# Attention's reciprocal as a logarithm and an exponential, and one vector-matrix product moved from TensorE to VectorE

## The reference

```python
q = xt @ Wq.T                                   # keys and values are q too
scores = scale * einsum('bhqd,bhkd->bhqk', qh, qh)
logits = (scores * cmask + (1.0 - cmask) * NEG) * rmask
attn = softmax(logits, axis=-1)
ctx = einsum('bhqk,bhkd->bhqd', attn, qh)
x = x + transpose(ctx @ Wo.T)
```

## Time and profile before

| | |
|---|---|
| median of 3 runs | 1603.24 us (1598.74 to 1605.35) |
| span of the profiled execution | 1599.3 us (its only time; the runs' median lies 3.9 us above) |
| TensorE, GpSimd, VectorE, ScalarE busy | 95%, 84%, 75%, 55% |
| mean granted TensorE clock | 0.981 |

### The profile page before, as it was taken

The page is one execution under the profiler, slowest core; times in us unless marked ns, Lnnn a source line. Parts: engine busy times, 40 slices in busy tenths (PEclk is TensorE's granted clock), DMA queues, the critical chain, the costliest instruction groups (busy, mean ns, idle before and its releaser), DMA issues. The chain is left out here.

```text
span 1599.3 us, 32587 instructions
## 1 busy us (share of the span) xinstructions
PE 1513.2 (95%) x10636; PEld 1185.6 (74%) x10636; DVE 1198.6 (75%) x2676; ACT 877.7 (55%) x2189; POOL 1336.3 (84%) x1078
## 2 busy tenths in 40 slices
PE   5789999999999999999999999999999999999985
PEld 4568777777777777777777777777777777777753
DVE  4487787878778787877878787787878778787753
ACT  4345556565655656565565656556565655656441
POOL 3377989898898989889898988989898898988875
PEclk9779999999999999999999999999999999999998
DMA  4423444544444454444445444444554444454411
GB/s 137 104 65 96 108 120 109 130 123 111 118 113 117 112 130 123 110 118 115 116 113 130 123 110 119 114 117 111 130 123 111 119 113 117 111 130 96 111 53 55
DMA packets 93809, 179.07 MB, mean 112 GB/s; under 512 B 24704, under 2 KB 24832, under 8 KB 93632
## 3 DMA queue, kind: packets, MB, share of 16 engines
q1 hardware_dynamic: 64448, 109.71, 29.2%
q0 software_dynamic: 29184, 67.17, 14.9%
HBM read 36.77 MB, written 33.55 MB: 44 GB/s over the span
## 5 line engine op out<-in xcount | busy, mean ns | idle before, releaser
L835 ACT ACTIVATE small_Pt<-scores,small_kbias 108x270 f32<-108x270 f32 x1280 | 550.9, 483 | 343.7 <-PE scores L1245 334.8
L985 DVE TENSOR_REDUCE small_mxp<-max_scores 108x1 f32<-108x270 f32 x1280 | 546.7, 435 | 250.7 <-PE max_scores L1226 228.9
L646 POOL TENSOR_TENSOR small_Pacc<-small_Pacc,small_Pt 108x540 f32<-108x540 f32 x384 | 520.8, 1356 | 122.3 <-ACT small_Pt L835 116.6
L1226 PE MATMUL max_scores<-small_ops 128*108 128x270 f32 x1280 | 420.1, 336 | 22.2 <-DVE small_mxp L985 21.6
L1257 PE MATMUL ctx_psum<-small_Pt,small_V 108*64 108x270 f32 x2560 | 317.5, 395 | 0.0
L1017 DVE RECIPROCAL small_rsum<-small_rsum 128x67 f32<-128x67 f32 (+1 forms) x512 | 240.8, 532 | 66.3 <-ACT small_rsum L771 66.3
L1242 PE MATMUL scores<-small_ops 128*108 128x270 f32 x1280 | 281.1, 294 | 8.7 <-ACT small_Pt L835 7.0
L1226 PEld LDWEIGHTS max_scores<-small_ops 128*108 128x108 f32 x1280 | 221.3, 175 | 89.9 <-issue 38.4
L1257 PEld LDWEIGHTS ctx_psum<-small_Pt,small_V 108*64 108x64 f32 x2560 | 187.4, 139 | 109.0 <-issue 4.6
L1245 PE MATMUL scores<-small_ops 128*108 128x270 f32 x1280 | 265.4, 289 | 0.0
L1242 PEld LDWEIGHTS scores<-small_ops 128*108 128x108 f32 x1280 | 193.5, 174 | 38.4 <-ACT small_Pt L835 20.1
(11 more groups left out here) (129 smaller groups left out, 2273.2 us busy)
## 6 DMA issues: line engine op xcount, KB each, us to landing
small_ops<-small_H SPq DMA_DIRECT2D x512, 135.0 KB, 2.5
small_ops<-small_L SPq DMA_DIRECT2D x256, 135.0 KB, 2.5
small_ops<-small_mrow SPq DMA_DIRECT2D x128, 2.1 KB
small_xg<-x_rows,small_idx POOLq DMA_INDIRECT x80, 3.9
small_xtail<-x_rows,small_idx POOLq DMA_INDIRECT x80, 5.0
out_rows<-small_xtail,small_idx POOLq DMA_INDIRECT x80, 3.7
out_rows<-small_xg,small_idx POOLq DMA_INDIRECT x80, 4.1
wqT_sb<-wqT SPq DMA_DIRECT2D x1, 1024.0 KB, 5.4
```

The lines of the kernel that those rows point to most:

```text
L646: nc.gpsimd.tensor_tensor(acc, other, t["Pt"][:R, p0], ALU.add).then_inc(pacc_step, 1)
L835: nc.scalar.activation(t["Pt"][:R, (NT * s + k) % f.NP, half, :], ST[(2 * (NT * h + k) + half) % 3][:R, 0:H], ACT.Exp, bias=t["kbias"][:R, ...
L985: nc.vector.tensor_reduce(t["mxp"][:R, h % 2, m // 2, m % 2:m % 2 + 1], MX[m % 2][:R, 0:H], AX.X, ALU.max).then_inc(mx_red, 1)
L1226: nc.tensor.matmul(MX[m % 2][:R, 0:H], ops[:, OPA, tile_cols(m // 2)], ops[:, OPB, half_cols(m % 2)], start=True, stop=True).then_inc(mx_r ...
```

## The change

Two things are changed in the `small` and `middle` forms.

The reciprocal 1/(s + tiny) becomes exp(-ln(s + tiny)) on ScalarE, two instructions, followed by a Newton step on VectorE: the product of the estimate with the sums, written back to the bank, then (product - 2) times the estimate. The sign that this leaves is taken out by the scale, whose two halves become scalar_tensor_tensor with -1. The misc bank of the sums is released by VectorE's second instruction instead of ScalarE's copy. One activation table set that holds both functions is loaded ahead.

w becomes four VectorE instructions, one for each 128 channels of the mean (a product, then three products with an addition), which sum G's rows by channel on each partition; TensorE then adds the 128 partitions up with one product with ones. VectorE's instructions stand at (7, 0) part 1 (one) and (7, 2) part 1 (three, ahead of the Newton step), TensorE's at (7, 3); in the last batch at (6, 3), two in each part and ahead of the scale half of that part, and at (7, 0).

```diff
-    ((6, 0), (6, 1), "proj", (5, 1)), ((7, 0), (7, 1), "proj", (6, 0)), ((7, 3), (7, 4), "w", 0)]
+    ((6, 0), (6, 1), "proj", (5, 1)), ((7, 0), (7, 1), "proj", (6, 0))]
-LAST_W_AT = ((6, 4), (7, 0))
+W_SUM_AT = [(7, 0, 1), (7, 2, 1), (7, 2, 1), (7, 2, 1)]
+W_AT = (0, (7, 3))
+LAST_W_SUM_AT = [(6, 3, 0), (6, 3, 0), (6, 3, 1), (6, 3, 1)]
+LAST_W_AT = (0, (7, 0))
-RECIPROCAL_AT = [(2, 1), (2, 1), (2, 1), (2, 1)]
+RECIPROCAL_AT = (2, 1)
...
+    for c, at in enumerate((W_SUM_AT if has_next else LAST_W_SUM_AT) if form.split else []):
+        table[at].append(("w_sum", c))
     for h in range(HEADS):
         if h > 0 or has_prev:
-            for quarter, at in enumerate(RECIPROCAL_AT if form.split else [(2, 1), (3, 0), (3, 1), (4, 0)]):
+            if form.split:
+                table[(h, *RECIPROCAL_AT)].append(("refine", 0))
...
+                    if f.split:
+                        nc.scalar.activation(t["rsum"][:], MB[bank][:, 0:H], ACT.Ln, bias=tiny[:, 0:1]).then_inc(logs_done, 1)
+                        act.wait_ge(logs_done, s + 1)
+                        nc.scalar.activation(t["rsum"][:], t["rsum"][:], ACT.Exp, scale=-1.0).then_inc(rsum_done, 1)
+                        return
...
+                if f.split:
+                    nc.scalar.add_instruction(mybir.InstLoadActFuncSet(
+                        name=nc.get_next_instruction_name(), act_func_set_id=EXP_AND_LN))
...
+                def refine(s, bank):
+
+                    dve.wait_ge(rsum_done, s + 1)
+                    nc.vector.tensor_tensor(MB[bank][:, 0:H], t["rsum"][:], MB[bank][:, 0:H], ALU.mult).then_inc(recip_step, 1)
+                    dve.wait_ge(recip_step, 2 * s + 1)
+                    nc.vector.scalar_tensor_tensor(out=t["rsum"][:], in0=MB[bank][:, 0:H], scalar=-2.0, in1=t["rsum"][:],
+                                                   op0=ALU.add, op1=ALU.mult).then_inc(recip_step, 1)
...
+                    if f.split:
+                        last = nc.vector.scalar_tensor_tensor(
+                            out=t["ctx"][pr:pr + DK, h // 2 % 2, cols], in0=t["rsum"][r0:r0 + DK, :], scalar=-1.0,
+                            in1=CT[r0:r0 + DK, 0:H], op0=ALU.mult, op1=ALU.mult)
...
+                def w_sum(b, c):
+
+                    if c == 0:
+                        dve.wait_ge(xbar_kept, b + 1)
+                        dve.wait_ge(g_kept, KD)
+                        at_least(dve, tail_added, NTAIL * b)
+                        at_least(dve, out_done, NT * b)
+                        nc.vector.tensor_scalar(t["w"][:], G[:, 0, :], t["xbarT"][:, 0:1], None,
+                                                ALU.mult).then_inc(w_sum_step, 1)
+                        return
+                    dve.wait_ge(w_sum_step, KD * b + c)
+                    nc.vector.scalar_tensor_tensor(out=t["w"][:], in0=G[:, c, :], scalar=t["xbarT"][:, c:c + 1],
+                                                   in1=t["w"][:], op0=ALU.mult, op1=ALU.add).then_inc(w_sum_step, 1)
...
                     elif name == "L":
-                        at_least(pe, rsum_done, HEADS * b + arg + 1)
+                        if f.split:
+                            at_least(pe, recip_step, 2 * (HEADS * b + arg) + 2)
...
+                    elif name == "w" and f.split:
+                        pe.wait_ge(w_sum_step, KD * (b + 1))
+                        nc.tensor.matmul(mb[:, 0:D], ones64[:, 0:1].to_broadcast([P, P]), t["w"][:],
+                                         start=True, stop=True).then_inc(w_ready, 1)
```

More of the change, by code:

```diff
@@ L33 @@
 NEG = -1e30
+EXP_AND_LN = 6
 SLOTS = 4
@@ L128, in misc_jobs @@
         for first, last, name, arg in PAIR_STEPS:
-            if (has_prev if name == "out" else name == "w" or arg[0] < PAIRS or has_next):
-                in_chunks(name, arg, *(LAST_W_AT if name == "w" and not has_next else (first, last)))
+            if has_prev if name == "out" else arg[0] < PAIRS or has_next:
+                in_chunks(name, arg, first, last)
+        part, at = W_AT if has_next else LAST_W_AT
+        whole(part, "w", 0, at)
         if has_next:
@@ L218, in vector_jobs @@
     table = {(h, k, a): [] for h in range(HEADS) for k in range(form.NT) for a in range(2)}
+    for c, at in enumerate((W_SUM_AT if has_next else LAST_W_SUM_AT) if form.split else []):
+        table[at].append(("w_sum", c))
     for h in range(HEADS):
         if h > 0 or has_prev:
-            for quarter, at in enumerate(RECIPROCAL_AT if form.split else [(2, 1), (3, 0), (3, 1), (4, 0)]):
+            if form.split:
+                table[(h, *RECIPROCAL_AT)].append(("refine", 0))
+            for quarter, at in enumerate([] if form.split else [(2, 1), (3, 0), (3, 1), (4, 0)]):
                 table[(h, *at)].append(("reciprocal", quarter))
@@ L1027, in scale @@
                     if half == 0:
-                        dve.wait_ge(recip_step, 4 * (s + 1))
+                        dve.wait_ge(recip_step, (2 if f.split else 4) * (s + 1))
                         if s == 0:
@@ L1039, in scale, with alone @@
                     r0, pr, cols = DK * half, DK * (h % 2), slice(half * H, half * H + H)
-                    last = nc.vector.tensor_tensor(
-                        t["ctx"][pr:pr + DK, h // 2 % 2, cols] if f.split else t["ctxT"][pr:pr + DK, h // 2, cols],
-                        t["rsum"][r0:r0 + DK, :], CT[r0:r0 + DK, 0:H] if f.split else t["ctxraw"][r0:r0 + DK, :], ALU.mult)
+                    if f.split:
+                        last = nc.vector.scalar_tensor_tensor(
+                            out=t["ctx"][pr:pr + DK, h // 2 % 2, cols], in0=t["rsum"][r0:r0 + DK, :], scalar=-1.0,
+                            in1=CT[r0:r0 + DK, 0:H], op0=ALU.mult, op1=ALU.mult)
+                    else:
+                        last = nc.vector.tensor_tensor(t["ctxT"][pr:pr + DK, h // 2, cols], t["rsum"][r0:r0 + DK, :],
+                                                       t["ctxraw"][r0:r0 + DK, :], ALU.mult)
                     if half == 1:
                         last.then_inc(ctx_done, 1)
-                def alone(name, arg, b, par, h):
-                    if name == "reciprocal":
+                def alone(name, arg, b, par, h, sums_bank=None):
+                    if name == "refine":
+                        refine(HEADS * b + h, sums_bank)
+                    elif name == "reciprocal":
                         reciprocal(HEADS * b + h, arg)
@@ L1130, in batch @@
                                 for name, arg in extras[h, k, a]:
-                                    alone(name, arg, b, par, h - 1)
+                                    alone(name, arg, b, par, h - 1, next((j[4] for j in table[h, 2] if j[1] == "L"), None))
                                 if f.split and not has_prev and a == 0 and (h, k) in HOT_ROW_AT:
@@ L1138, in tail @@
                         job(name, arg, bank, B, B % 2, HEADS * B - 1)
+                        if name == "L" and f.split:
+                            alone("refine", 0, B, B % 2, -1, bank)
                         if name == "L":
-                            for quarter in range(4):
+                            for quarter in range(0 if f.split else 4):
                                 alone("reciprocal", quarter, B, B % 2, -1)
@@ L1279, in bank_left @@
                     elif name == "L":
-                        at_least(pe, rsum_done, HEADS * b + arg + 1)
+                        if f.split:
+                            at_least(pe, recip_step, 2 * (HEADS * b + arg) + 2)
+                        else:
+                            at_least(pe, rsum_done, HEADS * b + arg + 1)
                     elif name == "out":
```

7 lines of the change are left out of this document (5 added, 2 removed).

## The result

The changed kernel takes 1709.19 us (median of 4 runs, 1708.6 to 1711.62), the kernel before 1602.32 in runs beside it: a ratio of 1.067, 95% interval 1.066 to 1.069. It is slower by 107 us, far outside the predicted range of 1587 to 1632. The profiled execution has a span of 1707.3 us, 108.0 more than before.

The account below looks back on a forecast made before the run. TensorE, busy 95%, was taken as the bound. To the 1599.3 us span it added 9 for 15 batches and 1.3 for the last: 1609.6, or 1613.5 as median; own range 1606 to 1621, eight in ten 1587 to 1632.

Parts of the forecast that it names:

- The reciprocal: Every head: VectorE saves 0.97 us, 124 us in all; sums about 0.53 us later on ScalarE; gain costed at nothing.
- The tensor_scalar's wait: Head 7's start: first product waits under GpSimd's addition of 718.14, ends near 719.8; head 6's sums slip 0.7 us.
- The second product's race: Head 7: second product runs 722.15 to 722.9, a hair ahead of GpSimd's addition of 722.29.
- the second product too loses its race: Rival, head 7 at 722.29: three full turns, a loss of 1.9 us a batch, 1633 us; chance 0.09.
- The two take turns: Products beside GpSimd's additions: the later one stands still, up to 1.85 us a product instead of 0.75.
- TensorE's saving: Head 7: one matmul pair of four stays, saving 2.56 us a batch, 41 us over 16, if nobody else were late.
- the products hide: Rival, head 7: TensorE gains up to GpSimd's 1.39 us of spare time a batch, 1584 us; chance 0.23.
- The last batch: Head 6: products between the scale halves meet additions, ScalarE's cast near 1559, head 7's exps 1.3 us later; +1.3.

Follow-up runs that it names:

- the run of the first product earlier: Changed kernel with w's first product moved from (7, 0) to (6, 4), where GpSimd adds nothing: 1699.27 us, ratio 1.062.
- one-gap run: Changed kernel with one gap on GpSimd in head 7, before the fourth of its six additions: 1685.69 us, ratio 1.051.
- four gaps: Changed kernel where each of GpSimd's four token sums in head 7 waits for the end of the addition issued before it: 1635.82 us, ratio 1.022.
- the version without collisions: Changed kernel with w's running sum in PSUM and all four products at (7, 2): 1588.62 us, again 1589.08, ratio 0.992.
- the run with the token sums moved: Kernel with the running sum in PSUM, GpSimd's four token sums moved from head 7 to heads 1 to 4 of the next batch: 1589.22 us.
- three products: Kernel with the running sum in PSUM, w's fourth product moved from VectorE to TensorE as one pair of matmuls: 1591.30 us, ratio 0.994.
- the kernels with moved sums: Token sums moved to heads 1 to 4 of the next batch: changed kernel 1619.99 us, running sum in PSUM 1589.22, that with fourth product on TensorE 1598.59.

## Why the prediction was wrong

**The reciprocal: right.** All its prices hold to 0.02 us but the Exp's, 0.43 for 0.48; alone it is worth nothing for the time, as costed, because TensorE sets the time. The one thing not seen is that it becomes worth 8 us in a version where VectorE's chain in head 7 matters.

**The tensor_scalar's wait: right.** It was put at an end of 0.3 us behind the addition of 718.14 with head 6's sums 0.7 late. It ended at 763.80 + 1.31 = 765.11, 0.29 behind the addition of 763.46, and the sums were 0.7 late. Alone it takes 0.48 to 0.49. The Trainium skill's rule (SBUF — State Buffer, Who interferes with whom), that a DVE op in a two-port mode is shut out for a whole GpSimd instruction, fits these numbers.

**The second product's race: wrong by 0.20 us, at a place with a margin of 0.14.** The prediction has it run "a hair ahead of the addition of 722.29". On the same clock (the tensor_scalar's 763.80 is its 718.56) it came at 722.16, as reckoned, but the addition at 722.10. A gather of GpSimd's ahead of it took 1.01 us (765.00, above) where it took 1.29 in the kernel before; the prediction had left GpSimd's clock as it was:

```profile
719.67 1.29 POOL L580 DMA_INDIRECT small_xg<-x_rows,small_idx  x1 [0.18 <-issue]
```

Why the gather is shorter was not tried. The rival "the second product too loses its race" named the lost race and held 0.09; the run of the first product earlier shows that even 0.07 ahead isn't enough. A race decided by 0.14 us, worked out over 4 us of chain, deserved about even chances.

**"The two take turns": the step that failed.** The cost of a lost race was taken as the rest of one addition and 0.55, so 1.85 us, from the earlier trace rows; the rival with the lost race was priced so too, 1.9 us a batch and 1633 us. It cost 8.05 us for the product and 7.5 a batch. In batches 0 to 13 the product that comes 0.04 to 0.06 us behind the first addition of an unbroken run is passed over by every addition of the run. The rows were read rightly and their place wrongly: in the earlier trace rows the first addition ends at 1565.03 + 1.51 = 1566.54 and the next starts at 1566.63. There is a gap of 0.09 us, and GpSimd had come out of a wait of 1.57 us. In head 7, where the price was used, and the text beside them say themselves that GpSimd goes from one addition to the next. The one-gap run shows what the difference is worth: with a gap of 0.07 us the product gets in there and nowhere before, and the two products behind it take 1.63 and 1.69 us, near the prediction's price. With four gaps all three do (1.84, 1.65 and 1.70); that kernel takes 1635.82, near the rival's 1633.

How the price grew to six additions is also shown: GpSimd stops only for lack of work, here with a wait of 6.57 us for exponentials, and that comes only when TensorE has stood idle for lack of w. What the prediction had as its worst case, a turn each, was a middle one.

**TensorE's saving: right as work, hardly to be had.** In the version without collisions 0.9 of the 2.56 us a batch arrive. The prediction's rival "the products hide" had up to 1.39 us from GpSimd's slack as its cap; the run with the token sums moved shows that GpSimd was not the cap (no change). It was not far from it: in one batch of the PSUM kernel its sums of head 7 are done at 725.48 + 1.34 = 726.82 and TensorE asks for them at 727.01, so 0.19 of the 1.39 are left. VectorE's chain is a cap (the reciprocal worth 8 us), TensorE's own work another (three products no better than four). Its time of 1584 was 5 us too low even for the kernel in which they do hide.

**The last batch: right mechanism, wrong size.** +3.1 us for +1.3: its products took 0.75, 1.87 and 1.69 us, in turns, and the tensor_scalar 0.49.

**The clock** was not in the sum at all: behind each standstill TensorE works at 1.2 GHz for 3.5 to 4.0 us or, in every second batch, for 5.5 to 6.0, which takes most of the saving of 2.56.

**Still open.** Why turns, once begun, go on without gaps: in the one-gap and four-gap runs and in batch 14 the additions behind the first are themselves held up (1.6 to 1.9 us instead of 1.3), and a product that waits behind such a one gets in. Whether being held up is the reason was not tried. Nor is it settled who is first when two starts are that close: a product 0.07 us ahead of an addition lost, while the product of 1572.36 in batch 14, 0.02 us behind the addition of 1572.34, took 0.74 us and the addition 1.89. That addition followed another without a gap (1571.04 + 1.34 = 1572.38), so a gap is not the only way in: a product that starts together with an addition in a run can win too.

## What to carry to other kernels

A price for two engines that shut each other out holds only for the pattern in which it was read: look whether the other engine's instructions there had a gap between them, and if they run back to back where the price will be used, price the wait up to the end of the run and not at one instruction. Better, leave the contest: with one operand in PSUM the same four products took 0.75 us each beside the same additions, and a loss of 7% became a gain of 0.8%. And where a step hangs on who starts first by a tenth or two of a us, give both outcomes real chances and price the bad one by what ends it.

## What the runs showed of the hardware

- A VectorE instruction with both tensors in SBUF that starts 0.06 us behind a GpSimd addition is not served next: it stood through six additions back to back, 8.05 us, and ended 0.56 us behind the last. The Trainium skill (SBUF — State Buffer, Who interferes with whom) has the loser blocked for the whole of the other's instruction; here it was blocked for six of them.
- A gap of 0.07 us in that run lets it in (4.36 us with a gap behind the third addition); from there the two engines take turns at 1.60 to 1.76 us each, without further gaps.
- It is not only the products: a 540-column subtraction of 0.71 us, also with both tensors in SBUF, took 5.63 beside a run that only the last batch of the kernels with moved sums had.
- With the second tensor in PSUM neither engine waits: 0.74 to 0.76 us beside additions of 1.29 to 1.34. The tensor_scalar gives up its short form for that, 0.74 for 0.48 us.
- In TensorE's wait of 6.6 us the granted clock falls from 1.00 to 0.50 (0.98 in the mean of 773 to 774, 0.50 from there), and it is still 0.50 for the first 3.6 us of the work behind the wait (777.2 to 780.8).
